# One transpose for the parts of all row maxima, and a mask of ones in place of the head blocks, in an attention stage

## The reference

```
qkv = x @ wi.T + bi
q, k, v = heads(...)                                   # 16 heads, 8 wide
scores = einsum('bhqd,bhkd->bhqk', q, k) / sqrt(8)
attn = softmax(scores, axis=-1)                        # the row maximum is subtracted before exp
o = einsum('bhqk,bhkd->bhqd', attn, v)
x = layernorm(x + o @ wo.T + bo)
```

## Time and profile before

| what | value |
|---|---|
| runs of the kernel | 565.91, 567.18, 567.09 us, median 567.09 |
| profiled execution | 565.99 us |
| its span (first to last instruction) | 564.2 us |
| mean granted TensorE clock in it | 0.968 |
| instructions | 14442 |
| TensorE busy (products) | 499.3 us, 88% |
| VectorE busy | 423.8 us, 75% |
| ScalarE busy | 393.3 us, 70% |
| GpSimd busy | 286.2 us, 51% |

### The profile page before, as it was taken

The page is one execution under the profiler, slowest core; times in us unless marked ns, Lnnn a source line. Parts: engine busy times, 40 slices in busy tenths (PEclk is TensorE's granted clock), DMA queues, the critical chain, the costliest instruction groups (busy, mean ns, idle before and its releaser), DMA issues. The chain is left out here.

```text
span 564.2 us, 14442 instructions
## 1 busy us (share of the span) xinstructions
PE 499.3 (88%) x4663; PEld 338.0 (60%) x4663; DVE 423.8 (75%) x1192; ACT 393.3 (70%) x1144; POOL 286.2 (51%) x511
## 2 busy tenths in 40 slices
PE   5998899999999999999789999999997867697880
PEld 3765566667767777765345656565564555576760
DVE  3589988888888888987455688787878768765652
ACT  3567688888888887787466778776876537476750
POOL 0587653322222222020345458887887375755673
PEclk9999999999999999999999999999999899978895
DMA  8700999999995000000100000101041043243310
GB/s 350 290 3 1 303 301 297 294 296 288 292 297 145 0 0 0 2 1 1 37 3 2 1 3 21 39 31 39 31 189 39 25 142 102 90 118 103 102 33 5
DMA packets 48535, 60.90 MB, mean 108 GB/s; under 512 B 2488, under 2 KB 45509, under 8 KB 47574
## 3 DMA queue, kind: packets, MB, share of 16 engines
q1 hardware_dynamic: 45686, 53.72, 32.7%
q0 software_dynamic: 2784, 6.37, 3.2%
HBM read 18.43 MB, written 42.10 MB: 107 GB/s over the span
## 5 line engine op out<-in xcount | busy, mean ns | idle before, releaser
L1619 DVE TENSOR_REDUCE nm<-SC 128x8 f32<-128x1024 f32 x64 | 75.4, 1219 | 29.8 <-PE SC L1115 29.4
L2146 ACT ACTIVATE room_p<-ST 128x512 f32<-128x512 f32 (+1 forms) x96 | 64.2, 742 | 23.8 <-PE ST L1133 23.8
L1515 DVE TENSOR_REDUCE room_w<-SC 128x512 f32<-128x2048 f32 x32 | 73.1, 2284 | 1.3 <-PE SC L945 1.3
L613 POOL TENSOR_TENSOR spread<-parts,units 128x48 bf16<-128x48 bf16 x32 | 8.8, 275 | 122.3 <-DVE parts L1490 122.3
L2053 ACT ACTIVATE room_w<-room_w,shift 128x128 f32<-128x128 f32 x128 | 50.0, 393 | 17.8 <-DVE shift L1524 17.8
L812 POOL DMA_INDIRECT out<-room_v,id_r x39 | 39.4, 1009 | 25.0 <-DVE room_v L1967 18.1
L2044 ACT ACTIVATE room_w<-ST,cv 128x128 f32<-128x128 f32 x128 | 36.6, 368 | 18.2 <-PE ST L960 18.1
L960 PEld LDWEIGHTS ST<-room_w 128*128 128x128 f32 x256 | 33.1, 191 | 15.3 <-issue 13.0
L2062 ACT ACTIVATE room_w<-room_w,inv 128x128 f32<-128x128 f32 x128 | 41.2, 410 | 0.0
L715 POOL DMA_INDIRECT sorted_rows<-room_w,slot_i x32 | 33.4, 1042 | 14.0 <-issue 9.7
L913 PE MATMUL ST<-room_w 128*128 128x136 f32 x256 | 40.2, 279 | 0.0
(11 more groups left out here) (307 smaller groups left out, 1367.3 us busy)
## 6 DMA issues: line engine op xcount, KB each, us to landing
sorted_rows<-w SPq DMA_DIRECT2D x8, 4290.0 KB, 38.4
room_v<-sorted_rows SPq DMA_DIRECT2D x39, 130.0 KB
x_t<-xT SPq DMA_DIRECT2D x2, 1024.0 KB, 8.2
ctx_t<-adj SPq DMA_DIRECT2D x1, 2048.0 KB, 16.8
room_w<-x SPq DMA_DIRECT2D x8, 256.0 KB, 3.0
room_w<-mask SPq DMA_DIRECT2D x1, 1536.0 KB
w<-weights SPq DMA_DIRECT2D x1, 1356.0 KB, 8.8
x_t<-w SPq DMA_DIRECT2D x1, 1032.0 KB, 5.0
```

Source lines behind the costliest of these rows:

```text
L1515: dve.tensor_reduce(logit[:, :, :], SC[:, :, :].rearrange("p b (i m) -> p b m i", i=TYPES), AX_X, ALU.max)\
L1619: dve.tensor_reduce(nm[:, v % 2, 2 * PER_R * pair:2 * PER_R * (pair + 1)], SC[:, 2 * pair:2 * pair + 2, :].rearrange("p r (i n) -> p (r i) ...
L2146: act.activation(ex[:, v % 2, first:last, :], ST[:, first:last, :], ACT.Exp)\
```

## The change

The parts of all 16 heads share one block of 128 columns: head h has columns 8h to 8h+2. One transpose turns the block, so that the parts of a head lie on its own 8 partitions, and 128 columns are evicted in place of 512. A strip then holds the parts of its four heads below each other, and a product of ones would add all four heads' parts to every head. So the constant `pick_head` takes the place of the ones: 32 rows a strip, one for each place i of a head in its strip, with ones on that head's 8 rows and zeros elsewhere. For each i and each strip a product of 32 rows by 128 columns adds the parts to the columns of that head: 16 products in place of four, each with its own weights. TensorE tells of the end after the last round of strips 1 and 3. VectorE makes `pick_head` once from `hmask`, and TensorE and VectorE wait for four constants in place of three. GpSimd's four operations write the same 16 elements a partition at other places. Three buffers are allocated on their own.

```diff
--- before.py
+++ after.py
@@ -207,17 +207,18 @@
 
         w2_s = Bf(128, EXPERTS * FF)
         v_a = Bf(128, 2, GB, VROW)
-        nmp = Bf(128, 2, PER_R, N, dt=BF16)
         q_s = Bf(128, 2, GT)
         k_s = Bf(128, 2, GT)
         o_n = Bf(128, 2, D)
         o_t = Bf(128, 2, N)
-        rhs_m = Bf(128, 2, GT, dt=BF16)
         o_raw = Bf(128, 2, GT)
         h_s = Bf(128, 2, GB, D + LOGITS)
         xn = Bf(128, GB, D)
         x1_g = Bf(128, GB, D)
         rows = Bf(128, 2, GB, ROW)
+        nmp = sb("nmp", [128, 2, N], BF16)
+        rhs_m = sb("rhs_m", [128, 2, N], BF16)
+        pick_head = sb("pick_head", [128, PER_R, N], BF16)
         nm = sb("nm", [128, 2, HEADS])
         nres = sb("nres", [128, HEADS])
         iq_s = sb("iq_s", [128, 1])
@@ -336,7 +337,7 @@
         X0, X1 = ST[:, 0, :], ST[:, 1, :]
         OT = SC[:, 0, :]
         OQ = SC[:, 1, :]
-        MT = SC[:, 2, 0:GT // 2].bitcast(BF16)
+        MT = SC[:, 2, 0:N // 2].bitcast(BF16)
         ON = SC[:, 3, 0:N]
         Y0, Y1 = ST[:, 0, :], ST[:, 1, :]
         HB = ST[:, 2, 0:D + LOGITS]
@@ -669,7 +670,7 @@
 
             pool.wait_ge(ctx_done, STEPS - G)
             pool.memset(v_a[:, :, :, :], 0.0).then_inc(S("va_zero"), 1)
-            pool.memset(nmp[:, :, :, :], 0.0).then_inc(S("va_zero"), 1)
+            pool.memset(nmp[:, :, :], 0.0).then_inc(S("va_zero"), 1)
             pool.wait_ge(S("va_zero"), 1)
             for par in range(2):
                 ones = v_a[:, par, :, 0:HEADS * VW].rearrange("p b (h c) -> p b h c", c=VW)[:, :, :, HD]
@@ -733,9 +734,8 @@
 
             def top_parts(v):
 
-                tops = nm[:, v % 2, :].rearrange("p (r i) -> p r i", r=ROWS_R)
-                rest = nres[:, :].rearrange("p (r i) -> p r i", r=ROWS_R)
-                part = lambda n: nmp[:, v % 2, :, :].rearrange("p i (r c) -> p r i c", r=ROWS_R)[:, :, :, n]
+                tops, rest = nm[:, v % 2, :], nres[:, :]
+                part = lambda n: nmp[:, v % 2, :].rearrange("p (h c) -> p h c", c=HD)[:, :, n]
                 pool.wait_ge(S("tops_ready"), 2 * (v + 1))
                 if v >= 2:
                     pool.wait_ge(S("mt_mm"), v - 1)
@@ -1128,18 +1128,18 @@
                     pe.matmul(ST[:, r, :], k_s[at, g % 2, b * N:(b + 1) * N],
                               q_m[at, g % 2, :, b * N:(b + 1) * N], start=True, stop=False)
                 pe.wait_ge(S("mt_out"), v + 1)
-                for r in range(ROWS_R):
-                    at = slice(STRIP * r, STRIP * (r + 1))
-                    mm = pe.matmul(ST[:, r, :], ones_h[at, :], rhs_m[at, v % 2, :], start=False, stop=True)
-                    if r % 2:
-                        mm.then_inc(S("st_mm"), 1)
+                for i in range(PER_R):
+                    for r in range(ROWS_R):
+                        at = slice(STRIP * r, STRIP * (r + 1))
+                        mm = pe.matmul(ST[:, r, i * N:(i + 1) * N], pick_head[at, i, :], rhs_m[at, v % 2, :],
+                                       start=False, stop=(i == PER_R - 1))
+                        if i == PER_R - 1 and r % 2:
+                            mm.then_inc(S("st_mm"), 1)
 
             def turn_tops(v):
 
                 pe.wait_ge(S("parts_chain"), 4 * (v + 1))
-                for i in range(PER_R):
-                    mm = pe.transpose(MT[:, i * N:(i + 1) * N], nmp[:, v % 2, i, :], ident_h[:, :])
-                mm.then_inc(S("mt_mm"), 1)
+                pe.transpose(MT, nmp[:, v % 2, :], ident_h[:, :]).then_inc(S("mt_mm"), 1)
 
             def weigh(v):
 
@@ -1265,7 +1265,7 @@
                     gate_folds()
 
             rounds(pe, step)
-            pe.wait_ge(S("halves_ready"), 3)
+            pe.wait_ge(S("halves_ready"), 4)
             for u in FLOW:
                 lower_banks_free(u)
                 if batch(u):
@@ -1782,10 +1782,12 @@
             dve.tensor_copy(before_h[:, :], C("before")).then_inc(S("halves_ready"), 1)
             dve.tensor_copy(ones_h[:, :], C("ones")).then_inc(S("halves_ready"), 1)
             dve.tensor_copy(base_h[:, :], C("base")).then_inc(S("halves_ready"), 1)
+            dve.tensor_copy(pick_head[:, :, :], C("hmask").unsqueeze(2).broadcast_to([128, PER_R, N]))\
+                .then_inc(S("halves_ready"), 1)
             dve.memset(cs[:, :], 0.0).then_inc(S("cs_zero"), 1)
             dve.memset(cs_h[:, :], 0.0).then_inc(S("cs_zero"), 1)
             dve.wait_ge(S("cs_zero"), 2)
-            dve.wait_ge(S("halves_ready"), 3)
+            dve.wait_ge(S("halves_ready"), 4)
             done_at = [0]
 
             def then(ins):
```

## The result

The changed kernel takes **573.07 us** (median of 572.02, 577.53, 572.13 and 574.0), beside 566.5 us of the kernel before, measured together with it (565.81 to 567.18). The ratio is 1.0126, with a 95% interval of 1.0087 to 1.0164: 1.3% slower. Forecast were 564.3 us and faster.

A forecast was written before the change was run, and what follows sets the result against it. Bound: the attention loop of addition, two exponentials, residual and TensorE in order. 20 passes at 0.16 us gained 3.2, seven value passes cost 0.4: net -2.8 us, forecast 564.3 us, range 562.3 to 568.0.

The forecast's parts named there:

- instructions: TensorE, whole kernel: 96 transposes go, 384 products come with loads, 576 instructions more; no cost beyond the addition's rounds.
- GpSimd ... 0: GpSimd's four operations on 128x16 elements stay as before: cost 0.
- Transposes, 4 to 1: Transposes of the maxima on the loop: 0.39 us becomes 0.22, a gain of 0.17 us a pass.
- Eviction: Eviction of the turned maxima, 512 to 128 columns: shorter, but TensorE doesn't wait for it, so worth nothing.
- The addition: Adding the maxima in 16 products: four rounds of 0.055 us, weight loads free, exponentials start 0.01 us later.
- Rival B: Weight loads set the pace of the addition's rounds: slower, up to +5.3 us (572.4) at 0.155 a round; chance 0.15.
- The scores behind it: Line 1115 after the addition: fp32 weight load less covered, start 0.06 us later, hidden in most passes by VectorE's reserve.
- Value passes: Seven passes that take out the next group's values: shorter transposes bring nothing, scores' delay adds 0.06 us each, 0.4 together.
- The mask: A VectorE copy of 128x512 ahead of the attention stage: hidden under waits for TensorE, without that cover 0.5 us once.
- The sum: 20 passes gain 0.16 us each, 3.2 us; seven value passes cost 0.4; net -2.8 us.
- Rival A: VectorE's maxima take over as the attention loop's bound: only 1.4 us gained, 565.7 us; chance 0.23 together with rival C.
- Rival C: The gain doesn't arrive in the total: 0 to 1.4 us gained, 565.7 to 567.1; chance 0.23 together with rival A.

The follow-up runs named there:

- change_again: The changed kernel measured once more, unaltered, beside the kernel before at 567.01 us: 573.79 us, ratio 1.0132.
- fourth series: Both kernels with GpSimd's scatters moved later, the last four behind the last pass: changed kernel 562.25 us, kernel before 564.05, beside the unaltered kernel before at 565.86.
- the second: Series with scatters made to wait for the next batch's addition: changed kernel 566.53 us, kernel before 566.44, beside the unaltered kernel before at 567.01.
- split16_again: The kernel before with only the addition cut into 16 products of 128 columns, beside the kernel before at 567.99 us: 577.29 us, ratio 1.0162.
- first series: Runs on chip 0 beside the kernel before at 548.64 us; that kernel with only its addition cut into 16 products took 550.27 us, ratio 1.0029.
- own_buffers: The kernel before with only `nmp` and `rhs_m` in places of their own, beside the kernel before at 548.64 us: 548.65 us, ratio 0.9999.

## Why the prediction was wrong

**The step that failed** is the one on instructions: "576 more on TensorE ... so nothing beyond the round", together with "GpSimd ... 0". I priced the instructions by what they cost the array, and there the price was right. I did not ask what else they pass through on the way: their completion has to reach ScalarE, and beside a scatter it comes up to 1.5 us late. By the forecast's own terms passes 12 to 26 should have been 10 x 0.16 - 4 x 0.06 = 1.4 us shorter. They were 7.4 longer, which is 8.8 us of difference. The profiled execution misses the forecast for it by 572.02 - 563.2 = 8.8 us as well, but that the two agree to the tenth is chance: 0.55 us of a later first addition, 0.35 of a smaller gain in passes 0 to 11 and 0.9 outside the span stand against 1.75 us that the time behind pass 26 gained beyond the forecast (in change_again it gained 0.3 in all). Nothing else of the size of the 8.8 was wrong. The scatters beside the addition stood in the timeline of before, but I had no rows on them, and the rivals held no mechanism at that place. The trace of the kernel before did contain a warning: ScalarE's idle time "remote" of 4.96 us, where a dense run of products meets a scatter.

*Transposes, 4 to 1* (0.17 gained on the loop): right, 0.22 us with the heads' transpose 0.05 behind it.

*Eviction* (worth nothing): right. It takes 0.28 us now, and neither before nor after does the addition wait for it.

*The addition* (0.055 a round, exponentials 0.01 later): right. The rounds are 56 ns apart, the group lasts 0.40 us, the exponentials come 0.01 later. **Rival B** falls with it: a round in which each load had to wait for the products in its strips would have been 0.155. The rule of the Trainium skill (TensorE: Matmul & The Clock Gate, "What overlaps and what doesn't"), that a load overlaps products in flight only when its row group differs, does not describe line 1134, where every round loads into strips that are in use. The result was slower, as rival B said, but not by its mechanism.

*The scores behind it* (0.06 later, hidden in most passes): right in size, 615 ns on average where they were 587. The profile shows it otherwise than forecast: line 1115 starts 0.22 us after the first product, not 0.27, and half of its products last 643 ns in place of 587. But "hidden" was wrong in half of the passes, and this is the term that was mis-sized. Where a piece of a projection follows the scores (u = 0, 3, 4, 7, ...), it starts when line 1115 has streamed, and the residual follows the piece; from the addition to the residual it is 2.21 us now and 2.15 before. Those passes went from 5.62 to 5.51, a gain of 0.11. The others gained 0.16 (5.81 to 5.65, 5.66 to 5.50).

*Value passes* (0.06 longer): right, 5.86 after 5.80. With the scatters moved those from 13 on take 5.91 to 6.04. There TensorE waits about 0.4 us in each for VectorE's additions (the row of line 1130 above); why these come later was not tried.

*The mask, GpSimd's parts*: nothing of them is seen. The first addition comes at 275.61 us (275.06 before), in change_again at 274.96.

*The sum.* By the same terms passes 0 to 11 should have given 9 x 0.16 - 3 x 0.06 = 1.3 us and gave 0.9. The whole change, freed from held signals, gives 1.8 us by the medians of the fourth series and nothing in the second, where 2.8 were forecast.

*Rival A* was not seen: in the passes without a scatter no weighing waits for VectorE's first maxima. *Rival C* neither: the attention stage itself got longer.

**What stays open** is the mechanism behind the held signals. Shown are the conditions (a scatter of GpSimd in progress or just starting, many TensorE instructions in a few tenths of a us) and the two moments of release, about 0.3 us after the scatter's end or 0.54 to 0.60 us after its start. That the products themselves are on time rests on the model of their ends and on the next ones being issued on time. Whether the signals share a path with the scatter's descriptors, and which, no run here says; nor were loads and products told apart, whose numbers grow together. There is no clean threshold either. In passes 12 to 27 the kernel before had up to 20 TensorE instructions starting within a scatter's own duration, and none of its additions was held; nor was the one of pass 30, with 41. With 8 products it were 28 in six passes, the first signal held by 0 to 0.73 us. With 16 products (changed kernel, split16_again) all were held by 0.09 us or more in which the scatter ended after the last product or at most 0.3 us before it. Among these are passes with only 4 and 11 instructions within the scatter, held by 1.26 and 1.14 us (pass 13 of the changed kernel, pass 12 of split16_again): there the addition ended as the scatter began, so what passes shortly before counts too. And in the first series 44 instructions within a scatter were held by less than 0.2 us. What makes the first series differ is open. It alone ran on chip 0, so the chip is the first candidate, but no chip was measured twice at different times except chip 11 (567.01 and 567.99 us), so chip and time can't be told apart. The kernel before was 18 us faster there. By the profile of own_buffers 17 of these lie behind pass 26, mostly in the experts' stage, where signals are held under GpSimd's writes of the outputs by up to 5.6 us in the first profile of the kernel before.

## What to carry to other kernels

Before cutting one TensorE instruction into many at equal streaming time, look at what runs on the other engines at that moment: count the engine's instructions per tenth of a us, and see whether a GpSimd indirect DMA overlaps them. If a consumer starts late though its producer was issued on time, compare the producer's modelled end with the semaphore's update, and see what ended just before it. Moving the transfer by a us can be worth more than the edit itself: on chip 11 it brought the changed kernel 7 us, where the edit itself promised under 3. But on chip 0 there was next to nothing to win, and for the kernel before nothing on chip 11.

## What the hardware showed that was not expected

A busy or idle figure of TensorE says nothing of when its completion becomes known: signals came up to 1.5 us late in the attention stage of the changed kernel (3.44 in the tail of the kernel before), with the array working on, since the following products were issued on time. Loads of 32x128 bf16 weights cost no time of their own even when every round of products changes them (56 ns a round), while the first fp32 loads behind a short round cost 56 ns. And one unchanged kernel took 548.6 us on one chip (0) and 566 to 568 in the series on two others (11 and 13), with the runs of a series within 1.2% of each other.
